# Decoder LSTM step with the doubled cell in PSUM and one transposed block per step; order of the first loads changed

## The chip, the cores and the metric

One core of a Trainium2 chip runs the whole program. The time is the device time of one execution in microseconds (us), the median of several runs. TensorE (PE) multiplies matrices into PSUM, PEld is its weight load, VectorE (DVE) and ScalarE (ACT) work on tiles in SBUF and PSUM, GpSimd (POOL) on tiles in SBUF, and SyncE (SP) issues the DMAs of this kernel. Each engine works through its own queue in order; semaphores tie the queues together.

## What is computed

```python
h = tok(x)                          # x: 16 x 1024 x 64; token mixing
h = h + attn(layernorm(h))          # LSTM encoder (both directions) and LSTM decoder
h = h + ffn(layernorm(h))           # 8 experts, the 2 best of each token

def tok(x):                         # q, k, v = x @ W + b
    y = ((d_gamma * (q @ k.T)) @ v) @ Wo + bo
    return where(y >= 0, y, prelu_a * y)

def step(carry, xw):                # of each LSTM, 1024 steps, 16 x 128 state
    h, c = carry
    i, f, g, o = split(xw + h @ U, 4, axis=-1)
    c = sigmoid(f) * c + sigmoid(i) * tanh(g)
    h = sigmoid(o) * tanh(c)
    return (h, c), h

h_fwd, h_bwd = lstm(x @ Wf + bf, Uf), lstm(x @ Wb + bb, Ub, reverse=True)
dec = lstm(broadcast(concat(h_fwd, h_bwd)) @ Wd + bd, Ud, return_sequences=True)
attn_out = dec @ Wo + bo
```

The experts compute gelu(x @ W1 + b1) @ W2 + b2, masked by the two best gate scores.

## The kernel before, in words

The program is four blocks that follow each other; an engine enters a block only when all engines have left the one before.

**Set-up** (`setup`, L163). SP issues the gamma matrix (L195), the weights of token mixing, `bo_col` and `a_col` (L202 to L204), four bias rows, and then 22 loads of weights for the later stages (`load_raw`, L208 to L230), which count on `m.s_raw`. TensorE turns gamma, ScalarE keeps it (L272), and VectorE splits the weights of token mixing into high and low halves and makes the bias rows (L290 to L299). VectorE and TensorE wait for `s_w`, which counts all small loads up to `a_col`.

**Token mixing** (`token_mixing`, L374) goes through the 16 batches. SP loads x of batches 0 and 1 (L446), then x of batch b + 2 and the store of h of batch b in turn (L448 to L452). ScalarE's `x_split` (L598) is the first operation on a batch's x. A batch's 16 places `t` interleave the main part (`gate`, L626), the preparation of the next batch (`prep`) and the layernorm of the last one (`post`). `bo_col` is read at L580 and `a_col` at L644. GpSimd meanwhile waits for all 22 weights (L457) and splits them (`split_weights`, L334); the encoder needs them.

**Encoder** (`encoder`, L815): two chains, forward and backward, take turns for 1024 steps.

**Decoder and experts** (`decoder_and_experts`, L934): one chain of 1024 steps, in 32 bodies of `BODY` = 32 steps, all unrolled. A step of the chain is: twelve products of 16 columns on TensorE (`pe_gates`: eight of the high half of h, L749, then four of the low half, L752), tanh of the gates (L760, L762) on ScalarE, terms (L775) and their sum, twice the cell (L781), on VectorE, tanh of the cell (L767) on ScalarE, which writes PSUM bank 3, and back on VectorE h as a float16 high half (L806), as float32 (L807) and the low half (L812). `dve_rest` (L795) has the output gate (L798) and `dve_half_cell` (L792), which halves the doubled cell for the next step's terms. `twice_cell` is an SBUF tile.

Beside the chain, the experts of the tokens that earlier bodies made are worked through in tiles of 32 steps' tokens. A tile j has places s = 0 to 63 and starts in the body after its own; in a body the tile of the body before is at places 0 to 31 and the one before that at 32 to 63. `pe_part`, `act_part`, `in_tanh` and `in_gates` say what an engine does at a place. `in_tanh` stands in VectorE's order before the high half, `in_gates` behind the low half. At s = 37 and 38, which are steps 5 and 6 of a body, TensorE turns the sums yT, two blocks each (L1137), one float32 block being two matmuls in the trace. VectorE reads them at s = 43 (L1316). After its tile's work in each step TensorE runs a number of products that nobody reads (`pe_idle`, L740; `idle_products`, L921), which keep it busy.

```python
    by_place = {0: 0, 1: 4, 2: 5, 19: 5, 20: 9}
```

gives that number for the steps in which tiles are in work, save steps 3 to 18, which have 10 or 13.

## Time and profile before

| what | value |
|---|---|
| median of 3 runs | 3925.51 us (3924.63 to 3928.59) |
| profiled run | 3921.38 us, span 3919.6 us |
| PE busy | 3750.3 us (96%) |
| PEld busy | 2749.2 us (70%) |
| DVE busy | 3139.5 us (80%) |
| ACT busy | 2391.9 us (61%) |
| POOL busy | 85.4 us (2%) |
| set-up, token mixing | 0 to 26.3, 26.3 to 398 us |
| encoder, decoder | 398 to 2141, 2141 to 3919.6 us |

Busy time is the time in which an engine had an instruction of its own; DMA-issuing and waiting don't count. TensorE's share holds the products that nobody reads (15583 of 61932 matmuls are of L740), so it is not a measure of useful work. PEclk in the windows is the granted share of 2.4 GHz. A row of the timeline has start, duration, engine, line, operation and tiles, how many instructions were merged, and in brackets the idle time of the engine before it with what ended it.

### The profile page before, as it was taken

The numbers are of one execution on the slowest core, as the hardware profiler recorded it, in microseconds if no ns is written. First come the engines' busy times: TensorE is split into PE (matmuls) and PEld (weight loads), VectorE is DVE, ScalarE is ACT, GpSimd is POOL, SyncE is SP. The second block draws the span as 40 slices with busy tenths as digits, with TensorE's granted clock in tenths as the row PEclk, the third lists the DMA queues.
The fourth block names the chain that finished last, engine by engine and source line by source line (L and its number), as shares of the span: only waits on it lengthen the run. The fifth ranks groups of instructions, "written<-read, shape, count | busy, mean of one in ns | idle before, by whom it ended". The sixth has DMA issues, their size and how long they took to land. (4 is left out here: it accounts for less than half of the span.)

```text
span 3919.6 us, 159989 instructions
## 1 busy us (share of the span) xinstructions
PE 3750.3 (96%) x61932; PEld 2749.2 (70%) x61932; DVE 3139.5 (80%) x21227; ACT 2391.9 (61%) x11882; POOL 85.4 (2%) x129
## 2 busy tenths in 40 slices
PE   7899999999999999999999899999999999999998
PEld 3333888888888888888888666666666666666664
DVE  6999899999999999999998677766777667776675
ACT  3232898888889889888887344444444443444443
POOL 6100000000000000000000000000000000000000
PEclk8999999999999999999999999999999999999999
DMA  3111000000000000000000000000000000000000
GB/s 91 22 25 23 3 3 3 3 3 3 3 3 3 3 3 3 3 3 3 3 3 4 4 8 8 8 6 6 8 8 8 6 7 7 8 8 6 6 8 7
DMA packets 49571, 34.01 MB, mean 9 GB/s; under 512 B 37661, under 2 KB 46877, under 8 KB 48806
## 3 DMA queue, kind: packets, MB, share of 16 engines
q1 hardware_dynamic: 48806, 23.77, 2.3%
q8 instruction: 485, 7.95, 0.8%
q14 instruction: 280, 2.29, 0.2%
HBM read 15.37 MB, written 8.39 MB: 6 GB/s over the span
## 5 line engine op out<-in xcount | busy, mean ns | idle before, releaser
L740 PE MATMUL bank<-xs,ident 128*128 128x128 f16 x15583 | 1415.1, 223 | 0.0
L740 PEld LDWEIGHTS bank<-xs,ident 128*128 128x128 f16 x15583 | 1010.2, 102 | 252.2 <-issue 229.8
L760 ACT ACTIVATE ifg_cell_dec<-bank 128x48 f32<-128x48 f32 x1024 | 215.2, 210 | 641.3 <-PE bank L752 641.3
L752 PE MATMUL bank<-enc_lo,u_hi 128*128 128x16 f16 x8192 | 530.1, 173 | 0.3 <-DVE enc_lo L812 0.3
L749 PE MATMUL bank<-enc_hi,u_lo 128*128 128x16 f16 x8192 | 527.8, 173 | 0.0
L775 DVE SCALAR_TENSOR_TENSOR terms_dec<-ifg_cell_dec 128x32 f32<-128x32 f32 x1024 | 197.1, 193 | 398.3 <-ACT ifg_cell_dec L760 387.2
L749 PE MATMUL bank<-enc_hi,u_hi 128*128 128x16 f16 x8192 | 501.6, 170 | 0.0
L749 PEld LDWEIGHTS bank<-enc_hi,u_lo 128*128 128x128 f16 x8192 | 338.4, 96 | 205.6 <-DVE enc_hi L806 171.2
L767 ACT ACTIVATE bank<-twice_cell_dec 128x16 f32<-128x16 f32 x1024 | 191.7, 187 | 402.4 <-DVE twice_cell_dec L781 402.4
L752 PEld LDWEIGHTS bank<-enc_lo,u_hi 128*128 128x128 f16 x8192 | 339.3, 96 | 67.9 <-DVE enc_lo L812 0.4
L749 PE MATMUL bank<-ring_hi,u_lo 128*128 128x16 f16 x4096 | 260.7, 172 | 102.3 <-DVE ring_hi L806 96.0
L749 PEld LDWEIGHTS bank<-enc_hi,u_hi 128*128 128x128 f16 x8192 | 349.5, 96 | 0.0
L786 ACT ACTIVATE out_gate_bwd<-tanh_o_bwd,encoder_half_scale 128x16 f32<-128x16 f32 x1024 | 315.1, 308 | 33.6
L786 ACT ACTIVATE out_gate_fwd<-tanh_o_fwd,encoder_half_scale 128x16 f32<-128x16 f32 x1024 | 315.1, 308 | 33.5
L854 PE MATMUL bank<-ones,bias 128*128 128x128 bf16 x1024 | 323.4, 316 | 0.0
L852 PE MATMUL bank<-xs,w_lo 128*128 128x128 f16 x1024 | 323.2, 316 | 0.0
L749 PEld LDWEIGHTS bank<-ring_hi,u_lo 128*128 128x128 f16 x4096 | 183.6, 97 | 181.4 <-DVE ring_hi L806 160.5
L850 PE MATMUL bank<-xs,w_hi 128*128 128x128 f16 x1024 | 278.1, 272 | 1.4 <-PEq L434 1.4
L752 PE MATMUL bank<-ring_lo,u_hi 128*128 128x16 f16 x4096 | 263.6, 173 | 0.6 <-DVE ring_lo L812 0.3
L749 PE MATMUL bank<-ring_hi,u_hi 128*128 128x16 f16 x4096 | 250.6, 170 | 0.0
L1128 PE MATMUL bank<-hid,w 128*64 128x512 f32 x448 | 240.2, 618 | 0.0
L767 ACT ACTIVATE bank<-twice_cell_bwd 128x16 f32<-128x16 f32 x1025 | 191.8, 187 | 53.9
(268 smaller groups left out, 7900.8 us busy)
## 6 DMA issues: line engine op xcount, KB each, us to landing
g_rows<-tok_d_gamma_batched_dram SPq DMA_DIRECT2D x8, 512.0 KB, 6.5
x_rows<-in_x_dram SPq DMA_DIRECT2D x16, 256.0 KB, 3.0
kept_h<-tok_ln_h SPq DMA_DIRECT2D x32, 128.0 KB, 2.1
res<-kept_h SPq DMA_DIRECT2D x32, 128.0 KB
out_dram<-sums SPq DMA_DIRECT2D x32, 128.0 KB
raw_wd<-in_L_attn_Wd_dram SPq DMA_DIRECT2D x2, 256.0 KB
raw_experts<-in_L_ffn_W_dram SPq DMA_DIRECT2D x2, 256.0 KB
raw_u<-in_L_attn_Uf_dram SPq DMA_DIRECT2D x1, 256.0 KB
```

Of the source, the lines that this page charges most:

```text
L740: nc.tensor.matmul(spare, m.ident16[:], m.xs[:, 0, :, :].rearrange("p b t -> p (b t)"), start=False, stop=True, skip_group_check=True)
L749: nc.tensor.matmul(z[k], w[:, g, :], h_hi, start=False, stop=False, skip_group_check=True)
L752: last = nc.tensor.matmul(z[k], m.u_hi[c.d][:, g, :], h_lo, start=False, stop=True, skip_group_check=True)
L760: nc.scalar.activation(c.ifg_cell[:, 0:3, :], ifg, ACT.Tanh, scale=1.0 / Z_SCALE).then_inc(c.s_t_ifg, 1)
L767: nc.scalar.activation(c.tanh_cell, c.twice_cell[:], ACT.Tanh, scale=0.5).then_inc(c.s_tanh_cell, 1)
L775: nc.vector.scalar_tensor_tensor(c.terms[:], c.ifg_cell[:, 0:2, :], 1.0, c.ifg_cell[:, 2:4, :], ALU.add, ALU.mult).then_inc(c.s_terms, 1)
L786: nc.scalar.activation(c.out_gate[:], c.tanh_o[:], ACT.Identity, scale=0.5 * X_SCALE, bias=half_scale).then_inc(c.s_out_gate, 1)
L850: nc.tensor.matmul(z, m.w_hi[d][:, g, :], x, start=(k in (0, 3)), stop=False, skip_group_check=True)
L852: nc.tensor.matmul(z, m.w_lo[d][:, g, :], x, start=False, stop=False, skip_group_check=True)
L854: nc.tensor.matmul(z, m.lstm_bias[d][:, GATE_FROM[g], :], m.ones3[:].rearrange("p (b t) -> p b t", b=B), start=False, stop=False, skip_gro ...
L1128: mm(y_bank[0:D, :], m.w2[:, e, :], hid[:, e % 2, :], start=False, stop=False, skip_group_check=True)
```

## The change

1. In the decoder alone, `twice_cell` becomes columns 16 to 31 of PSUM bank 3, beside the cell's tanh in columns 0 to 15. VectorE's sum writes it there; ScalarE's tanh and VectorE's halving read it there.
2. In the decoder, the halving no longer stands behind the output gate but between h in float32 (L807) and the low half (L812).
3. The four blocks of yT are turned at s = 37, 38, 39 and 40, one each.
4. In step 19 of a body with tiles TensorE runs 2 products that nobody reads instead of 5.
5. x of batches 0 and 1 is loaded in the set-up behind the four bias rows. `bo_col`, `a_col` and the 22 weights are issued at the start of token mixing, ahead of x of batch 2; the first readers of `bo_col` and `a_col` wait for a semaphore of their own.

```diff
+def load_x(nc, sp, m, b, k):
+    sp.dma_start(m.x_rows[k][:], m.a["x"][b, 0].rearrange("(c p) d -> p c d", p=P)).then_inc(m.s_x[k], 16)
+def load_weights(nc, sp, m):
+    a = m.a
+    for k in range(2):
+        sp.dma_start(m.bo_col[k * D:(k + 1) * D, :], a["L0_tok_bo"][:, None]).then_inc(m.s_cols, 16)
+    sp.dma_start(m.a_col[:], a["L0_tok_prelu_a"][None, :].broadcast_to([P, 1])).then_inc(m.s_cols, 16)
...
+N_RAW = 16 * 22
@@ -199,36 +243,11 @@
-                for k in range(2):
-                    load(m.bo_col[k * D:(k + 1) * D, :], a["L0_tok_bo"][:, None])
-                load(m.a_col[:], a["L0_tok_prelu_a"][None, :].broadcast_to([P, 1]))
                 for k, name in enumerate(("bq", "bq", "bk", "bk")):
                     load(raw_mix[:, k * D:(k + 1) * D], a["L0_tok_" + name][None, :].broadcast_to([3, D]), s_b, n_b)
...
+                for b in range(2):
+                    load_x(nc, sp, m, b, b)
@@ -434,27 +452,23 @@
-                for b in range(2):
-                    load(b, b)
+                load_weights(nc, sp, m)
                 for b in range(B):
                     if b + 2 < B:
                         sp.wait_ge(s_xs, b + 1)
-                        load(b + 2, b % 2)
+                        load_x(nc, sp, m, b + 2, b % 2)
                     store_h(b)
@@ -577,6 +591,8 @@
                         act.wait_ge(s_av, NT * (b + 1))
+                        if b == 0:
+                            act.wait_ge(m.s_cols, 48)
@@ -641,6 +657,8 @@
                         dve.wait_ge(s_y, b + 1)
+                        if b == 0:
+                            dve.wait_ge(m.s_cols, 48)
@@ -715,20 +733,21 @@
-    def __init__(self, sb, sem, d, name, cell_bank):
+    def __init__(self, sb, sem, d, name, cell_bank, twice_in_bank=False):
         self.d = d
         self.tanh_cell = cell_bank[:, 0:B]
+        self.twice_cell = cell_bank[:, B:2 * B] if twice_in_bank else sb(f"twice_cell_{name}", [P, B], F32)[:]
@@ -789,15 +808,14 @@
-def dve_rest(nc, dve, c, n, sums):
+def dve_out_gate(nc, dve, c, n):
 
     dve.wait_ge(c.s_t_o, n + 1)
     nc.vector.tensor_scalar(c.out_gate[:], c.tanh_o[:], 1.0, 0.5 * X_SCALE, ALU.add, ALU.mult
                             ).then_inc(c.s_out_gate, 1)
-    dve_half_cell(nc, dve, c, sums)
@@ -922,7 +940,7 @@
-    by_place = {0: 0, 1: 4, 2: 5, 19: 5, 20: 9}
+    by_place = {0: 0, 1: 4, 2: 5, 19: 2, 20: 9}
@@ -940,7 +958,7 @@
-        c = Chain(sb, sem, 2, "dec", m.bank[3])
+        c = Chain(sb, sem, 2, "dec", m.bank[3], twice_in_bank=True)
@@ -1130,14 +1148,14 @@
-                    if s in (37, 38):
+                    if 37 <= s < 37 + QS:
 
                         if s == 37:
                             pe.wait_ge(s_yT, j + 1)
-                        for blk in range(2 * (s - 37), 2 * (s - 37) + 2):
-                            last = mm(pre_bank[0][:, blk * D:(blk + 1) * D], yT[:, blk * P:(blk + 1) * P],
-                                      m.ident[0:D, 0:D], start=(blk == 0), stop=True, skip_group_check=True)
-                        if s == 38:
+                        blk = s - 37
+                        last = mm(pre_bank[0][:, blk * D:(blk + 1) * D], yT[:, blk * P:(blk + 1) * P],
+                                  m.ident[0:D, 0:D], start=(blk == 0), stop=True, skip_group_check=True)
+                        if blk == QS - 1:
                             last.then_inc(s_yt, 1)
@@ -1359,11 +1377,12 @@
                         dve_terms(nc, dve, c, n)
                         dve_sum(nc, dve, c, n)
-                        dve_rest(nc, dve, c, n, n + 1)
+                        dve_out_gate(nc, dve, c, n)
                         part(in_tanh, tiles, step)
                         dve.wait_ge(c.s_tanh_cell, n + 1)
                         dve.wait_ge(c.s_out_gate, n + 1)
                         dve_hidden(nc, dve, c, n, h_at(ring_hi, n))
+                        dve_half_cell(nc, dve, c, n + 1)
                         dve_hidden_low(nc, dve, c, n, h_at(ring_hi, n), h_at(ring_lo, n))
                         part(in_gates, tiles, step)
```

## Rows read from the trace of the kernel before

**Rows 1.** Window, decoder: us; PE, PEld, DVE, ACT, POOL busy; clock; DMA; GB/s.

```profile
2141.10:3881.30 1740.20, 1636.83 (x24968) 1142.34 (x24968) 1217.75 (x8279) 699.48 (x3472) 0.00 (x0) 0.99 0.03 7
```

**Rows 2.** Timeline of ScalarE in a plain step of the decoder, and the next step's start.

```profile
3757.67 0.21 ACT L760 ACTIVATE ifg_cell_dec<-bank 128x48 f32<-128x48 f32 x1 [0.82 <-PE bank L752]
...
3758.35 0.19 ACT L767 ACTIVATE bank<-twice_cell_dec 128x16 f32<-128x16 f32 x1 [0.39 <-DVE twice_cell_dec L781]
...
3759.36 0.21 ACT L760 ACTIVATE ifg_cell_dec<-bank 128x48 f32<-128x48 f32 x1 [0.22 <-PE bank L752]
```

**Rows 3.** Timeline of VectorE in the same step, from the sum on.

```profile
3758.14 0.17 DVE L781 TENSOR_TENSOR twice_cell_dec<-terms_dec 128x16 f32<-128x16 f32 x1
...
3758.57 0.17 DVE L806 TENSOR_TENSOR ring_hi<-out_gate_dec,bank 128x16 f16<-128x16 f32 x1
3758.66 0.16 DVE L807 TENSOR_TENSOR h_dec<-out_gate_dec,bank 128x16 f32<-128x16 f32 x1
3758.85 0.18 DVE L812 TENSOR_TENSOR ring_lo<-h_dec,ring_hi 128x16 f16<-128x16 f32 x1
```

**Rows 4.** Source view of ScalarE's lines: shortest/median/longest ns, first and last start.

```profile
L767 ACT ACTIVATE bank<-twice_cell_dec x1024: 187/187/188, 2144.1 to 3881.6; 128x16 f32<-128x16 f32 x171
...
L762 ACT ACTIVATE tanh_o_dec<-bank x1024: 178/178/179, 2143.4 to 3881.0; 128x16 f32<-128x16 f32 x171
...
L583 ACT ACTIVATE tok_ln_dev<-tok_ln_var x16: 208/208/209, 72.3 to 392.4; 128x8 f32<-128x8 f32 x16
```

**Rows 5.** Timeline of step 5 of a body, ScalarE and TensorE.

```profile
3728.90 0.21 ACT L760 ACTIVATE ifg_cell_dec<-bank 128x48 f32<-128x48 f32 x1 [0.31 <-PE bank L752]
...
3730.62 0.21 ACT L760 ACTIVATE ifg_cell_dec<-bank 128x48 f32<-128x48 f32 x1 [0.85 <-PE bank L752]
...
3729.01 0.66 PE L1138 MATMUL bank<-ident,ff_yT 64*128 64x64 f32 x4
```

**Rows 6.** Timeline of step 19 of the same body, ScalarE and TensorE.

```profile
3752.54 0.21 ACT L760 ACTIVATE ifg_cell_dec<-bank 128x48 f32<-128x48 f32 x1 [0.21 <-PE bank L752]
...
3754.29 0.21 ACT L760 ACTIVATE ifg_cell_dec<-bank 128x48 f32<-128x48 f32 x1 [0.88 <-PE bank L752]
...
3753.54 0.45 PE L740 MATMUL bank<-xs,ident 128*128 128x128 f16 x5
3753.83 0.25 PE L749 MATMUL bank<-ring_hi,u_lo 128*128 128x16 f16 x4
...
3754.03 0.24 PE L752 MATMUL bank<-ring_lo,u_hi 128*128 128x16 f16 x4
```

**Rows 7.** Window on the second of ten stretches of the decoder at half clock.

```profile
3130.20:3133.60 3.40, 3.40 (x54) 3.40 (x52) 2.44 (x20) 0.80 (x6) 0.00 (x0) 0.51 0.00 0
```

**Rows 8.** Timeline of SP in the set-up and at token mixing's start.

```profile
12.38 0.36 SPq L191 DMA_DIRECT2D raw_u<-in_L_attn_Uf_dram  x1
...
25.43 0.27 SPq L191 DMA_DIRECT2D raw_b<-in_L_ffn_b_dram  x1
26.30 4.98 SPq L438 DMA_DIRECT2D x_rows<-in_x_dram  x3
```

**Rows 9.** Timeline of ScalarE in the set-up and at token mixing's start.

```profile
16.29 0.19 ACT L275 COPY bv<-bv 64x3 f32<-64x3 f32 x1 [0.67 <-PE bank L260]
...
29.41 0.63 ACT L598 ACTIVATE x_split<-x_rows 128x512 f16<-128x512 f32 x1 [1.61 <-DMA x_rows<-in_x_dram]
```

**Rows 10.** Timeline of VectorE, its last operation in the set-up.

```profile
21.59 0.48 DVE L331 TENSOR_TENSOR bias<-left 3x320 bf16<-3x320 f32 x1
```

**Rows 11.** Timeline of GpSimd's first split, and of a small VectorE operation.

```profile
27.57 0.54 POOL L310 TENSOR_SCALAR raw_u<-raw_u 128x128 f32<-128x128 f32 x1 [23.68 <-DMA raw_b<-in_L_ffn_b_dram]
...
105.89 4.20 DVE L677 TENSOR_SCALAR tok_ln_t<-tok_ln_t 128x8 f32<-128x8 f32 x1
```

**Rows 12.** Windows from x_split to x_split, two batches of token mixing.

```profile
81.71:120.81 39.10, 23.63 (x121) 8.05 (x120) 36.91 (x38) 6.72 (x12) 33.34 (x15) 0.83 0.06 14
120.81:141.38 20.57, 20.57 (x123) 7.51 (x121) 19.06 (x36) 6.75 (x13) 0.00 (x0) 1.00 0.12 27
```

More of the change, by code:

```diff
@@ L156, in build @@
             m.s_raw = raw_sem("raw_loaded")
+            m.s_cols = raw_sem("columns_loaded")
+            m.s_b2 = raw_sem("b2_zeroed")
+            m.x_rows = [raw_sb(f"x_rows{k}", [P, NB, D], F32) for k in range(2)]
+            m.s_x = [raw_sem(f"x_loaded{k}") for k in range(2)]
             setup(nc, m)
@@ L160, in build, with load_raw @@
         decoder_and_experts(nc, m)
+def load_x(nc, sp, m, b, k):
[5 more added lines that the diff above has]
+    sp.dma_start(m.a_col[:], a["L0_tok_prelu_a"][None, :].broadcast_to([P, 1])).then_inc(m.s_cols, 16)
+    def load_raw(dst, src, scattered=False):
+        sp.dma_start(dst, src, allow_slow_non_contiguous=scattered).then_inc(m.s_raw, 16)
+    for d, u in enumerate((a["L0_attn_Uf"], a["L0_attn_Ub"], a["L0_attn_Ud"])):
+        load_raw(m.raw_u[d][:], u)
+    for d, w in enumerate((a["L0_attn_Wf"], a["L0_attn_Wb"])):
+        load_raw(m.raw_w[d][0:D, :], w)
+        load_raw(m.raw_w[d][D:2 * D, :], w)
+    for d in range(2):
+        load_raw(m.raw_wd[d][:], a["L0_attn_Wd"][H * d:H * (d + 1), :])
+    load_raw(m.raw_wo[:], a["L0_attn_Wo"])
+    for k in range(2):
+        load_raw(m.raw_wg[k * D:(k + 1) * D, :], a["L0_ffn_Wg"])
+        load_raw(m.raw_w1[k * D:(k + 1) * D, :, :], a["L0_ffn_W1"].rearrange("e d h -> d e h"))
+    load_raw(m.w2[:], a["L0_ffn_W2"].rearrange("e h d -> h e d"))
+    load_raw(m.b1[:], a["L0_ffn_b1"].rearrange("e h -> h e"), scattered=True)
+    at = 0
+    for name in ("attn_bf", "attn_bb", "attn_bd", "attn_bo", "ffn_bg"):
+        b = a["L0_" + name]
+        load_raw(m.raw_b[:, at:at + b.shape[0]], b[None, :].broadcast_to([3, b.shape[0]]))
+        at += b.shape[0]
+    sp.wait_ge(m.s_b2, 1)
+    load_raw(m.raw_b2[E:2 * E, 0, :], a["L0_ffn_b2"])
+N_RAW = 16 * 22
 def setup(nc, m):
@@ L386, in token_mixing @@
     with ctx:
-        x_rows = [sb(f"x_rows{k}", [P, NB, D], F32) for k in range(2)]
+        x_rows, s_x = m.x_rows, m.s_x
         x_split = sb("x_split", [P, NB, 2 * D], F16)
@@ L402, in token_mixing @@
         ln = Layernorm(sb, "tok_ln_")
-        s_x = [sem(f"x_loaded{k}") for k in range(2)]
         s_xh, s_xs, s_xt, s_xk, s_vo, s_vk, s_tile, s_hi, s_lo = (sem(n) for n in (
@@ L436, in _ @@
             def _(sp):
-                def load(b, k):
-                    sp.dma_start(x_rows[k][:], a["x"][b, 0].rearrange("(c p) d -> p c d", p=P)).then_inc(s_x[k], 16)
                 def store_h(b):
@@ L711 @@
 class Chain:
-    def __init__(self, sb, sem, d, name, cell_bank):
+    def __init__(self, sb, sem, d, name, cell_bank, twice_in_bank=False):
         self.d = d
         self.tanh_cell = cell_bank[:, 0:B]
+        self.twice_cell = cell_bank[:, B:2 * B] if twice_in_bank else sb(f"twice_cell_{name}", [P, B], F32)[:]
         self.ifg_cell = sb(f"ifg_cell_{name}", [P, 4, B], F32)
         self.terms = sb(f"terms_{name}", [P, 2, B], F32)
-        self.twice_cell, self.tanh_o, self.out_gate, self.h = (
-            sb(f"{part}_{name}", [P, B], F32) for part in ("twice_cell", "tanh_o", "out_gate", "h"))
+        self.tanh_o, self.out_gate, self.h = (
+            sb(f"{part}_{name}", [P, B], F32) for part in ("tanh_o", "out_gate", "h"))
         (self.s_z_ifg, self.s_z_o, self.s_t_ifg, self.s_t_o, self.s_terms, self.s_out_gate, self.s_twice,
@@ L729, in start @@
     def start(self, nc, own):
-        own.link(nc.vector.memset(self.twice_cell[:], 0.0))
+        own.link(nc.vector.memset(self.twice_cell, 0.0))
         nc.vector.memset(self.ifg_cell[:, 3, :], 0.0).then_inc(self.s_cell, 1)
```

40 lines of the change are left out of this document (8 added, 32 removed).

## The prediction

> **What bounds the kernel now.** I read the windows by stage first. Token mixing, encoder and decoder follow one another, and the decoder takes 1740.2 us of the 3919.6 us span [rows 1]. The diff touches two places: the decoder's step, and the order of loads around the set-up. The encoder keeps its instructions, and its tiles stay where they were; I put it at no change.
>
> In the decoder I read one step on three engines. ScalarE starts two successive tanh of the gates 1.69 us apart [rows 2]. 1024 steps at 1.69 us are 1730 us, so the loop through time is the stage. The loop runs so: gates' tanh (L760), terms (L775), their sum (L781), tanh of the cell (L767), hidden state high (L806) and in float32 (L807), its low half (L812), then TensorE's four products of the low half (L752), then the next gates' tanh. TensorE looks 94% busy [rows 1], but most of that is filler (L740). In the plain step the sum starts at 3758.14 and lasts 0.17, the cell's tanh starts at 3758.35 and lasts 0.19, and the high half starts at 3758.57: every link starts 0.03 to 0.04 after the end of the one before [rows 2, 3]. So a nanosecond off any of these durations is a nanosecond off the step, as long as TensorE is not what comes last.
>
> **Part 1, the doubled cell in PSUM.** The sum now writes PSUM, the cell's tanh and the halving (L792) read PSUM. ScalarE's tanh has three forms in the trace: from SBUF to PSUM 16 columns 187 ns, from PSUM to SBUF 16 columns 178, from SBUF to SBUF 8 columns 208 [rows 4]. The 48-column gates' tanh takes 0.21 and the 16-column one 0.178, so 32 columns are 0.03 and 8 columns some 7 ns [rows 2, 4]: SBUF to SBUF with 16 columns would be 215. Reading PSUM thus saves 215 - 178 = 37 ns where the output is SBUF; writing PSUM saves 28. If the savings added, PSUM to PSUM would take 150. They may overlap: the bounds for the tanh are 141 (a saving of 46, some more than the larger of the two) and 187 (none). I take 154, a saving of 33, a little below the sum of the parts.
>
> No row shows VectorE writing PSUM. Nearest are its reads: the high half has an input in PSUM and takes 0.17, as the sum with both in SBUF does [rows 3]; for VectorE one memory is as near as the other when it reads. I take 0 for the write, and bound it by -10 ns (the 0.17 of the sum against the 0.16 of L807) and by +37, ScalarE's largest gap turned round. Together: 33 ns a step, bounds 56 and -4. 1024 x 33 = 33.8 us.
>
> ScalarE's reading agrees with a rule that I set beside the rows: the Trainium skill (VectorE: DVE Perf Modes, section on the TRN2 errata) gives ScalarE 224 cycles from SBUF and 172 from PSUM, 43 ns at its 1.2 GHz; by that the 33.8 would be 44. The same table gives VectorE 62 cycles (65 ns) more from PSUM than from SBUF, which the 0.17 of L806 against the 0.17 of L781 contradicts.
>
> **Part 2, the halving moves.** It leaves the gap between out_gate and the high half and stands between L807 and L812. Where it was it cost nothing: it ran beside the tanh, and the high half started 0.22 after it, on the tanh's end [rows 3]. Its steps with an operation of in_tanh have the same gap, now with more room. Where it goes there is a gap too: L812 starts 0.20 after L807, because it waits for L807's end, while VectorE issues two such small operations 0.09 apart (L806 to L807) [rows 3]. The halving would start 0.09 behind L807 and let L812 go 0.18 behind it, so 0.02 stays spare: cost 0. Its result is wanted by the next terms, some 0.7 us later. Behind it queue L812 and all of in_gates; who waits for L812 is TensorE, on the path. That is the thin place.
>
> **Part 3, one block of transposes a step.** Now steps 5 and 6 of a body carry two blocks each. Step 5 takes 1.72 us from tanh to tanh, against 1.69; the four matmuls of its two blocks last 0.66 us, at about 0.13 each, 0.26 a block [rows 5]. TensorE then reaches the gates late. The median excess over the bodies is 34 ns in step 5 and 18 in step 6. A block less takes 0.26 away, more than either lateness; both excesses go. Steps 7 and 8 get the block; their filler ends some 0.5 us before the high half is there, so 0.26 is hidden. 30 bodies x 52 ns = 1.6 us. The sum of sums (L1316, step 43) comes three steps after the last block: no cost.
>
> **Part 4, three fillers fewer in step 19.** That step takes 1.75 us, 62 ns above the others. Five fillers last 0.45, so one is 56 ns, and the gates' first product starts 0.29 behind the start of the five [rows 6]. Against the chain (0.24 + 0.23 + 0.21 + 0.22 + 0.17 + 0.06 = 1.13 from tanh to first product if TensorE is free, all from [rows 2, 3] but the last, which is the wait's own) it starts at 1.29: 0.16 late. Three fillers are 0.168. The excess goes: 31 bodies x 62 ns = 1.9 us.
>
> **Where TensorE takes over.** The eight products of the high half take 0.20 [rows 6], and those of the low half can't start until 0.35 after the high half's end, so TensorE may start up to about 0.15 behind that end at no cost. The rest are medians over the bodies, each taken as in [rows 5, 6] from a step's L806, L749 and the two L760 around it: late by 0.144, step 2 loses 4 ns; late by 0.191, step 5 loses 34; the excess is the lateness less 0.157. A chain that is 33 ns shorter makes each TensorE-late step later by 33: steps 23 and 31 (now 0.132) then lose 8 each, step 2 loses 20, the others with 0.10 or 0.09 nothing. 36 ns x 31 = 1.1 us given back. **Decoder: 33.8 + 1.6 + 1.9 - 1.1 = 36.2 us.** With 56 ns it is 57.6, with 0 it is 3.5.
>
> **Part 5, the granted clock.** Ten times in the decoder, from 2642.0 to 3676.3 us, the clock is granted at 1.2 GHz instead of 2.4 for 3.4 us [rows 7]. All ten begin in step 6, right behind both pairs of transposes, and each makes that step 0.47 to 0.72 us longer, 6.2 us in all. The transposes use 64 rows and 64 columns. Spread over four steps, with the fillers of steps 5 and 6 no longer pushed back, that thin stretch is gone: 6.2 us, bounds 0 and 6.2.
>
> **Part 6, the loads.** Before, SP issues bo_col and a_col, then 22 weights from 12.38 to 25.70, and the next block starts at 26.30 with x's load, for which ScalarE waits until 29.41 [rows 8, 9]. After, x is issued from about 10.5, and the set-up ends with VectorE's last bias row, now 22.07 [rows 10]. That moves up too: a_col was the last load waited for. ScalarE stood idle 0.67 before L275 [rows 9], so the gain is 0.67 at most; I take 0.6, and the set-up ends at 21.45. With 0.60 between blocks (25.70 to 26.30) token mixing starts at 22.05. ScalarE's table load and first operation come first; it waited 1.61 for x behind them [rows 9]. x_split starts at 22.05 + (29.41 - 1.61 - 26.30) = 23.55 against 29.41: **5.9 us**.
>
> What is moved behind: the three columns and 22 weights issue from 22.05 to about 37.2; GpSimd, which began 2.1 us after the last issue (27.57), begins at 39.1, 11.5 us later, and ends near 128, long before the encoder at 398. On SP's queue, x of batch 2 now stands behind them, issued at 37.3 and landed at 40.1; ScalarE wants it at 52.2 (12 us of cover, the whole cost if that were gone). The first store of h (66.4) is not reached. bo_col lands near 25 and is read near 57. GpSimd's long operations block small VectorE ones: a scale of 8 columns takes 4.20 us beside one [rows 11], and the batch under them takes 39.10 us against 20.57 for the next [rows 12]. They shift by 11.5 us late and the batches by 5.9 early; about as many small operations meet them. I put it at 0, between -5 and +6.
>
> **Sum.** 36.2 + 6.2 + 5.9 = 48.3. The profiled run took 3921.4 us (span 3919.6), and comes to 3873.1. The median of the runs shown is 4.1 higher, 3925.5; on it: 3877.2.
>
> **The rivals.** *A: VectorE pays for PSUM what ScalarE saves.* With +37 on the sum a step gains -4 ns, the decoder loses 4.1 and keeps 3.5, so 3925.5 + 0.6 - 12.1 = 3914. For it: no row shows the write. Against: the equal reads. The Trainium skill (ScalarE: Activation LUTs, where it compares destinations) has this rule: "ScalarE is closer to PSUM, VectorE is closer to SBUF." No row here shows its second half for a write. Chance 0.17.
>
> *B: TensorE is the bound in the 14 steps with late products.* If their margin were not 0.157 but what they use now, 13 of them would gain nothing: 13 x 33 x 31 = 13.3 us less, 3891. Against: step 23, late by 0.132, is as short as the rest. Chance 0.06.
>
> *C: the low half slips, and it is slower.* If VectorE doesn't issue L812 until the halving has ended, L812 starts 0.09 + 0.17 + 0.03 = 0.30 after L807, not 0.20: 99 ns, less 33, are 66 ns a step, 67.6 us; less 15.6 for the other parts, 3978. It decides from a slip of 48 ns. For it: L812 is on the path and has 20 ns to spare. Against: L807 is issued 0.09 after L806, not after its end. Chance 0.07.
>
> *D: the change does less than it says*: the half clock stays, or the blocked batch grows: 6 us each, 3883 to 3890; these are inside the forecast's case.
>
> **How the numbers follow.** Forecast 0.64 (3858 to 3893), A 0.17, B 0.06, C 0.07, something else 0.06, split between faster and slower. The range goes from the larger saving (57.6 + 6.2 + 5.9 = 69.7, so 3856) to A: 3857 to 3914. The likeliest case's own range is 3858 to 3893. 0.2% (7.9 us, about what a measurement of this kernel tells from no change) puts the line at 3917.6: faster 0.86, same 0.05, slower 0.09.
>
> **What would show it.** L767 at about 154 ns (178 or more: part 1 is wrong); L781 still 174, and ScalarE starting 0.21 behind it (0.24 is A); L812 0.20 behind L807 (0.30 is C); steps 5, 6 and 19 as short as the rest, near 1.655; no half clock after a transposing step; first x_split at 23.5; the third batch still near 39 us. The prediction is wrong if the write isn't near 0, or if a different VectorE operation ends last in the step.

## The result, and the profile after

| | before | after |
|---|---|---|
| median of the runs timed side by side, us | 3925.07 (4 runs, 3919.37 to 3928.59) | 3901.52 (4 runs, 3894.48 to 3902.35) |
| ratio, 95% interval | 1 | 0.9933 [0.9917, 0.9948] |
| profiled execution, us; its span | 3921.38; 3919.6 | 3894.48; 3892.7 |
| mean granted TensorE clock | 0.986 | 0.992 |
| first x_split starts, us | 29.41 | 23.36 |
| encoder's first gates' tanh | 403.54 | 394.34 |
| decoder, first to last gates' tanh | 1737.58 | 1719.25 |

The kernel is 23.6 us faster by the medians and 26.9 by the two profiled spans, where 48.3 had been forecast. Each part gained as its sign said, and the total was half. 3901.5 lies inside the whole range (3857 to 3914) and above the likeliest case's own (3858 to 3893).

The first row of the page after answers to the table that stands ahead of the prediction (engine, busy us, share of the span, instructions):

```profile
PE 3752.8 (96%) x61839; PEld 2740.7 (70%) x61839; DVE 3054.7 (78%) x21227; ACT 2367.2 (61%) x11882; POOL 86.9 (2%) x129
```

The window on the decoder after, columns as in [rows 1]: it is 17.9 us shorter than [rows 1], and ScalarE is busy 25 us less for the same 3472 instructions.

```profile
2132.50:3854.80 1722.30, 1639.04 (x24874) 1135.86 (x24874) 1134.95 (x8281) 674.80 (x3472) 0.00 (x0) 1.00 0.03 7
```

**The plain step.** Timeline of ScalarE after (start, duration, engine, line, output and input, idle time before and what ended it), which answers to [rows 2]:

```profile
3730.35 0.21 ACT L779 ACTIVATE ifg_cell_dec<-bank 128x48 f32<-128x48 f32 x1 [0.23 <-PE bank L771]
...
3731.04 0.17 ACT L786 ACTIVATE bank<-bank 128x16 f32<-128x16 f32 x1 [0.40 <-DVE bank L800]
...
3732.02 0.21 ACT L779 ACTIVATE ifg_cell_dec<-bank 128x48 f32<-128x48 f32 x1 [0.82 <-PE bank L771]
```

Timeline of VectorE in the same step, which answers to [rows 3]:

```profile
3730.82 0.18 DVE L800 TENSOR_TENSOR bank<-terms_dec 128x16 f32<-128x16 f32 x1
...
3731.24 0.17 DVE L824 TENSOR_TENSOR ring_hi<-out_gate_dec,bank 128x16 f16<-128x16 f32 x1 [0.16 <-ACT bank L786]
3731.32 0.16 DVE L825 TENSOR_TENSOR h_dec<-out_gate_dec,bank 128x16 f32<-128x16 f32 x1
3731.41 0.17 DVE L811 TENSOR_SCALAR ifg_cell_dec<-bank 128x16 f32<-128x16 f32 x1
3731.52 0.18 DVE L830 TENSOR_TENSOR ring_lo<-h_dec,ring_hi 128x16 f16<-128x16 f32 x1
```

Gates' tanh to gates' tanh takes 1.67 where it took 1.69. From the sum's start to the tanh of the cell it is now 0.22 (0.21 before), from there to the high half 0.20 (0.22 before). The halving (L811) stands 0.09 behind the float32 hidden state, and the low half still starts 0.20 behind that. The source views give the nanoseconds (shortest/median/longest; first and last start), the tanh (L786) and the sum (L800), with the encoder's unchanged pair as a yardstick in the same run:

```profile
L786 ACT ACTIVATE bank<-twice_cell_fwd x1024: 187/187/188, 395.0 to 2129.1; 128x16 f32<-128x16 f32 x171
L786 ACT ACTIVATE bank<-bank x1024: 168/168/168, 2135.9 to 3855.1; 128x16 f32<-128x16 f32 x171
```

```profile
L800 DVE TENSOR_TENSOR twice_cell_fwd<-terms_fwd x1024: 174/175/178, 394.8 to 2128.9; 128x16 f32<-128x16 f32 x171
...
L800 DVE TENSOR_TENSOR bank<-terms_dec x1024: 182/182/185, 2135.7 to 3854.9; 128x16 f32<-128x16 f32 x171
```

The tanh has lost 19 ns (187 to 168) and the sum has gained 8 (174 to 182). That leaves about 10 ns a step: the median step is 1675 ns, where it was 1685.

**Steps 5 and 19.** ScalarE's gates' tanh of steps 5, 6 and 7 of a body, and of steps 19 and 20 of the same one. They answer to [rows 5, 6]; each step is now as long as a plain one, 1.67:

```profile
3757.15 0.21 ACT L779 ACTIVATE ifg_cell_dec<-bank 128x48 f32<-128x48 f32 x1 [0.33 <-PE bank L771]
3758.82 0.21 ACT L779 ACTIVATE ifg_cell_dec<-bank 128x48 f32<-128x48 f32 x1 [0.82 <-PE bank L771]
3760.50 0.21 ACT L779 ACTIVATE ifg_cell_dec<-bank 128x48 f32<-128x48 f32 x1 [0.82 <-PE bank L771]
...
3780.60 0.21 ACT L779 ACTIVATE ifg_cell_dec<-bank 128x48 f32<-128x48 f32 x1 [0.23 <-PE bank L771]
3782.27 0.21 ACT L779 ACTIVATE ifg_cell_dec<-bank 128x48 f32<-128x48 f32 x1 [0.82 <-PE bank L771]
```

**The loads.** SP's queue after, which answers to [rows 8]:

```profile
10.71 1.04 SPq L168 DMA_DIRECT2D x_rows<-in_x_dram  x2
21.96 1.12 SPq L175 DMA_DIRECT2D bo_col<-in_L_tok_bo_dram  x2
...
36.18 0.27 SPq L179 DMA_DIRECT2D raw_b<-in_L_ffn_b_dram  x1
36.49 0.39 SPq L168 DMA_DIRECT2D x_rows<-in_x_dram  x1
```

Then ScalarE's and VectorE's last operations of the set-up and the first of token mixing, and GpSimd's first; they answer to [rows 9 to 11]:

```profile
15.69 0.19 ACT L294 COPY bv<-bv 64x3 f32<-64x3 f32 x1 [0.24 <-PE bank L279]
...
20.98 0.48 DVE L350 TENSOR_TENSOR bias<-left 3x320 bf16<-3x320 f32 x1
...
23.36 0.61 ACT L614 ACTIVATE x_split<-x_rows 128x512 f16<-128x512 f32 x1
...
38.56 0.54 POOL L329 TENSOR_SCALAR raw_u<-raw_u 128x128 f32<-128x128 f32 x1 [34.66 <-DMA raw_b<-in_L_ffn_b_dram]
```

x is in the queue at 10.71, ScalarE no longer waits for it, and the first x_split starts at 23.36, 6.05 us earlier. GpSimd starts 11.0 later. The windows from x_split to x_split answer to [rows 12] (same columns): the blocked batch and the next one. The blocked one is now the fifth interval instead of the fourth.

```profile
95.34:132.61 37.27, 24.47 (x122) 8.18 (x121) 35.71 (x38) 6.73 (x12) 32.23 (x14) 0.82 0.07 15
132.61:153.06 20.45, 20.45 (x122) 7.46 (x121) 19.06 (x36) 6.74 (x12) 0.00 (x0) 1.00 0.12 26
```

And the timeline's row for VectorE's worst operation of 8 columns in the blocked one, usually 0.17 us:

```profile
118.32 4.20 DVE L695 TENSOR_SCALAR tok_ln_t<-tok_ln_t 128x8 f32<-128x8 f32 x1
```

GpSimd's row beside it starts before it and ends at 122.50; VectorE's ends at 122.52:

```profile
118.16 4.34 POOL L349 TENSOR_SCALAR bias_left<-bias_part,ident 3x1608 f32<-3x1608 bf16 x1
```

**The balance by the two traces**, in us of span, forecast beside it. The decoder's rows are sums over its steps from the second body on, of what each took beyond the median step:

| part | forecast | measured |
|---|---|---|
| median step, 1023 steps | -33.8 | -10.2 (1685 to 1675 ns) |
| steps 5, 6 and 19, less what TensorE gives back | -2.4 | -3.2 |
| steps under a half-clock stretch | -6.2 | -6.7 (6.8 to 0.1) |
| single steps more than 0.1 us longer than the median | 0 | +1.6 (13 to 23 of them) |
| loads, first x_split | -5.9 | -6.05 |
| intervals of token mixing | 0 | -2.7 |
| end of token mixing, encoder, tail and rounding | 0 | +0.3 |
| sum | -48.3 | -26.9 |

### The profile page after: what moved, and what is told of

Same layout as the page of the kernel before. It is cut to its first block and busy times, and to the rows that moved or that the text cites. A ratio compares the mean times of both kernels' runs of the same rounds, so it can differ in the third digit from the quotient of the medians.

```text
span 3892.7 us, 159805 instructions
## 1 busy us (share of the span) xinstructions
PE 3752.8 (96%) x61839; PEld 2740.7 (70%) x61839; DVE 3054.7 (78%) x21227; ACT 2367.2 (61%) x11882; POOL 86.9 (2%) x129
## 5 line engine op out<-in xcount | busy, mean ns | idle before, releaser
L759 PE MATMUL bank<-xs,ident 128*128 128x128 f16 x15490 | 1397.8, 221 | 0.0
L759 PEld LDWEIGHTS bank<-xs,ident 128*128 128x128 f16 x15490 | 994.6, 101 | 256.3 <-issue 230.0
L786 ACT ACTIVATE bank<-bank 128x16 f32<-128x16 f32 x1024 | 172.0, 168 | 411.7 <-DVE bank L800 411.7
L805 ACT ACTIVATE out_gate_fwd<-tanh_o_fwd,encoder_half_scale 128x16 f32<-128x16 f32 x1024 | 315.1, 308 | 33.6
L824 DVE TENSOR_TENSOR ring_hi<-out_gate_dec,bank 128x16 f16<-128x16 f32 x1024 | 174.7, 171 | 147.9 <-ACT bank L786 133.4
```

The lines of the kernel that those rows point to most:

```text
L759: nc.tensor.matmul(spare, m.ident16[:], m.xs[:, 0, :, :].rearrange("p b t -> p (b t)"), start=False, stop=True, skip_group_check=True)
L786: nc.scalar.activation(c.tanh_cell, c.twice_cell, ACT.Tanh, scale=0.5).then_inc(c.s_tanh_cell, 1)
L805: nc.scalar.activation(c.out_gate[:], c.tanh_o[:], ACT.Identity, scale=0.5 * X_SCALE, bias=half_scale).then_inc(c.s_out_gate, 1)
L824: tt(h_hi, c.out_gate[:], c.tanh_cell, ALU.mult).then_inc(c.s_hi, 1)
```

## The experiments

Two theories were set against each other for the missing 21 us. **Theory 1:** the two savings of the tanh overlap, and VectorE pays some nanoseconds to write PSUM; the other parts do what was forecast. **Theory 2 (the rival):** the step gained more, and another wait took it back: the moved halving, or TensorE. Two more questions were why the half clock went, and what GpSimd's later start does. Each comparison is with runs of the kernel before on the same chip. The kernels whose names begin with p_ have a part of the change alone, the others start from after. Medians are of all executions of a kernel; every row and every count of steps or stretches is of its one profiled execution.

**The doubled cell in PSUM and the moved halving alone (p_psum), and the moved halving alone (p_half).**

```
 # p_half: before, with the halving behind the hidden state
-                        dve_rest(nc, dve, c, n, n + 1)
+                        dve_out_gate(nc, dve, c, n)
                         dve_hidden(nc, dve, c, n, h_at(ring_hi, n))
+                        dve_half_cell(nc, dve, c, n + 1)
                         dve_hidden_low(...)
 # p_psum: the same, and
-        c = Chain(sb, sem, 2, "dec", m.bank[3])
+        c = Chain(sb, sem, 2, "dec", m.bank[3], twice_in_bank=True)
```

> The kernel before with the decoder's doubled cell in PSUM and the halving between L807 and L812; transposes, filler and loads as before. Theory (a step gets shorter by what the cell's tanh saves less what the sum pays): tanh 168 ns, sum 182 ns, a plain step 1.675 us instead of 1.685, so about 10 us less, minus what steps 5, 6, 19, 2, 23 and 31 give back because TensorE is late there; 3915 to 3917. Rival (the gain comes from moving the halving, not from PSUM): the step is 1.675 also with the doubled cell in SBUF, see p_half. The half clock after the pairs of transposes stays under both theories, in about as many bodies.

> The kernel before with only the halving moved between L807 and L812, the doubled cell still in SBUF. Theory: nothing moves, tanh 187 ns, L812 0.198 us after L807, step 1.685 us. Rival (the move itself is worth the 10 ns): step 1.675 us. Rival C of the prediction (the low half slips): L812 0.3 us after L807 and a step of 1.78.

p_psum: 3917.09 us (10 runs) against 3923.7 of before (25 runs), ratio 0.9988 [0.9978, 0.9997], at the upper end of what was expected. The tanh takes 168 ns, the sum 182, the median step 1676. Ten half-clock stretches stay, as in before, all in step 6. p_half (one run): 3925.8, tanh 187, sum 174, low half 198 ns behind the float32 state, median step 1685. So the step's 10 ns come from PSUM alone, and moving the halving costs the plain step nothing. It does cost something else: the number of single steps more than 0.1 us longer than the median, half-clock ones aside, goes from 13 in before to 26 in p_half and 25 in p_psum, and what they take from 3.4 us to 5.7 and 5.8. That is the larger part of why p_psum's decoder is only 6.4 us shorter, not 9.2 to 10.2 (9 to 10 ns by 1023); 0.6 us more goes to steps 5, 6 and 19, where TensorE is late. The single long steps are looked at under the encoder's experiment.

**One block of transposes per step alone (p_turns), and the change with the pairs put back (a_pairs).**

```
 # shortened. p_turns: before, with the change's turns (a_pairs: the reverse, in after)
-                    if s in (37, 38):
+                    if 37 <= s < 37 + QS:
-                        for blk in range(2 * (s - 37), 2 * (s - 37) + 2):
+                        blk = s - 37
```

> The kernel before with only the four blocks of yT turned one a step (s = 37 to 40); step 19 keeps its 5 fillers, the chain its SBUF tile. Theory (the pairs of transposes are what the half clock follows): none of the ten stretches at half clock is left, steps 5 and 6 are as short as the plain ones, step 19 still 1.747: 6.2 + 1.6 = 7.8 us less. Rival (the shorter step or the other order of loads moved the bodies against the clock's decisions): some of the ten stay and only 1.6 us go.

> The changed kernel with yT turned in pairs again (s = 37, 38); all else as changed. Theory (the half clock went because three edits act together: blocks spread, a shorter step, another time of the bodies): with the pairs back, stretches at half clock follow step 6 again in several bodies, steps 5 and 6 are 40 and 25 ns longer than the plain 1.675, and the kernel takes 6 to 9 us more than the changed one. Rival (it was the shorter step and the loads alone, the blocks don't matter to the clock): no stretch at half clock in the decoder, 2 us more.

p_turns: 3923.05 us (10 runs), ratio 0.9998 [0.9989, 1.0007]. Steps 5 and 6 are plain again where the clock is full (1.689 and 1.687 against 1.718 and 1.702). But five half-clock stretches stay, and all begin in step 6 although no step carries a pair. The window on one of them (columns as in [rows 7]):

```profile
3242.20:3245.60 3.40, 3.40 (x42) 3.26 (x40) 2.63 (x21) 0.66 (x4) 0.00 (x0) 0.50 0.00 0
```

Timeline of ScalarE's gates and TensorE's transposes around it:

```profile
3241.57 0.43 PE L1138 MATMUL bank<-ident,ff_yT 64*128 64x64 f32 x2
3241.65 0.21 ACT L760 ACTIVATE ifg_cell_dec<-bank 128x48 f32<-128x48 f32 x1 [0.82 <-PE bank L752]
...
3243.51 0.69 PE L1138 MATMUL bank<-ident,ff_yT 64*128 64x64 f32 x2
3243.59 0.21 ACT L760 ACTIVATE ifg_cell_dec<-bank 128x48 f32<-128x48 f32 x1 [1.07 <-PE bank L752]
...
3246.00 0.21 ACT L760 ACTIVATE ifg_cell_dec<-bank 128x48 f32<-128x48 f32 x1 [1.55 <-PE bank L752]
```

The granted clock is 0.50, which is the 1.2 GHz level, and steps 6 and 7 last 1.94 and 2.41 us. One stretch now costs 0.98 us, where it cost about 0.62 with the pairs: a block of step 7 falls under the half clock too (0.69 us for its two instructions instead of 0.43). Expected were 7.8 us less, or 1.6 by the rival. The profiled decoder is 3.0 us shorter, and the median over the executions moves by 0.65 us, with an interval (3.5 us less to 2.7 more) that rules out the 7.8 and not the 1.6. The stretches stay, as the rival has it. a_pairs: 3901.45 us (4 runs), 0.9952 [0.9935, 0.9968], six stretches in step 6 again, profiled decoder 5.6 us longer than after's. Of it 3.7 are the stretches and 1.9 the late steps 5 and 6. By the medians a_pairs is 3.9 us slower than after_again, less than the 6 to 9 that were expected.

**The change with the doubled cell back in SBUF (a_sbuf), and again as it is (after_again).**

```
 # a_sbuf
-        c = Chain(sb, sem, 2, "dec", m.bank[3], twice_in_bank=True)
+        c = Chain(sb, sem, 2, "dec", m.bank[3])
```

> The changed kernel with the decoder's doubled cell in SBUF again; halving, blocks, fillers and loads as changed. Theory: tanh 187, sum 174, step 1.685, 10 us more than the changed kernel from the step, and some stretches at half clock back, as in the kernel before with only the blocks spread, 3 us more; 3911 to 3915. Rival (the step's length has no part in the half clock): exactly the 10 us, 3911, no half clock in the decoder.

> The changed kernel itself, beside the versions below and beside the kernel before on the same chip. Theory: 0.993 of the kernel before, no stretch at half clock in the decoder between its first and last body, third to fifth batch of token mixing together about 19 us above 3 x 20.45. Rival (that no half clock stands in the decoder was one lucky execution): two to six such stretches and a mean granted clock of 0.988 over the executions.

a_sbuf: 3911.04 us (10 runs), 0.9978 [0.9969, 0.9988]. Its profiled execution was the slowest of the ten (3919.70), so its rows are less typical than the others'. Tanh 187, sum 175, median step 1688 (3 ns more than before's, for which no row gives a reason). Five half-clock stretches are back, all in step 6, and they cost 5.6 us, although no step carries a pair of transposes. after_again: 3897.51 (4 runs), 0.9942 [0.9925, 0.9958], median step 1675, one stretch.

One stretch at the start of the second body (6.8 us, in p_psum 10.2) is in every kernel, the prediction's ten don't count it, and nothing here moves it. From the third body to the last, before has 10 stretches and p_psum 10; p_half, p_turns and a_sbuf have 5, p_loads and a_pairs 6; after has none and after_again one. Neither the shorter step alone (p_psum) nor the spread turns alone (p_turns) takes them away, and with either missing (a_pairs, a_sbuf) five or six are back. The two together do. The unprofiled executions bear it out: taken over all of a kernel's executions, the mean granted clock has its median at 0.991 and 0.990 in after and after_again, at 0.988 in a_pairs and a_sbuf, and at 0.986 to 0.987 in before, p_psum, p_turns, p_half and p_loads. Why is open: in every kernel each of these stretches begins in step 6, but most bodies pass it at full clock. In before they come in series 54.6 us apart, which is the length of a body with a stretch in it (one without takes 54.0). That points to how the body falls against something periodic, and this is argued, not shown.

**The loads alone (p_loads).**

```
 # p_loads: after, with the decoder's turns, fillers, halving and SBUF cell of before
 ...
-    by_place = {0: 0, 1: 4, 2: 5, 19: 2, 20: 9}
+    by_place = {0: 0, 1: 4, 2: 5, 19: 5, 20: 9}
```

> The kernel before with only the loads changed: x of batches 0 and 1 in the set-up, the two columns and 22 weights at token mixing's start. Theory: the first x_split at 23.4 us instead of 29.4, the encoder's first tanh of the gates at 394.3 instead of 403.5, 9 us less. Rival (the set-up gives 6 and the rest of the 9 is chance of one execution): 6 us less.

3917.31 us (10 runs), 0.9985 [0.9976, 0.9994], 6.4 us less than before; the interval goes from 2.4 to 9.4 us and so excludes neither the 9 nor the rival's 6. In the profiled execution x_split starts at 23.02, 6.4 us earlier than in before, and the encoder's first tanh at 395.49, 8.0 us earlier. The other 1.7 us are in token mixing's intervals: together they took 315.8 to 317.2 us in the four kernels with the old order of loads and 313.7 to 315.1 in the eight with the new one and GpSimd's work uncut.

**A second halving (a_two_halves).** It adds one instruction whose result nobody reads.

```
                         dve_half_cell(nc, dve, c, n + 1)
+                        nc.vector.tensor_scalar(c.spare[:], c.twice_cell, 0.5, None, ALU.mult)
                         dve_hidden_low(...)
```

> The changed kernel with a second halving, into a tile that nobody reads, right behind the first, between L807 and L812. Theory (VectorE issues such operations about 0.085 apart whatever their length, and the place between h and its low half holds one but not two): L812 starts 3 x 0.085 = 0.26 us after the float32 write instead of 0.198, a step of 1.735, 60 us more in all. Rival (the place holds any number, since the low half waits for something else): no difference. Other rival (each waits for the one before to end): L812 at 0.45 and 250 us more.

3943.56 us (one run), 46.0 more than after_again, where 60 were expected; decoder 1764.80 against 1719.73. Timeline of VectorE in one step:

```profile
3001.28 0.16 DVE L826 TENSOR_TENSOR h_dec<-out_gate_dec,bank 128x16 f32<-128x16 f32 x1
3001.37 0.17 DVE L812 TENSOR_SCALAR ifg_cell_dec<-bank 128x16 f32<-128x16 f32 x1
3001.45 0.16 DVE L1387 TENSOR_SCALAR spare_dec<-bank 128x16 f32<-128x16 f32 x1
3001.53 0.17 DVE L831 TENSOR_TENSOR ring_lo<-h_dec,ring_hi 128x16 f16<-128x16 f32 x1
```

VectorE issues these 0.08 to 0.09 apart, and the low half starts 0.25 behind the hidden state instead of 0.20: with one operation in the gap there is room, with two there isn't. The median step grows by 38 ns: 49 of later start, less 11 by which the low half itself is shorter (164 instead of 175 ns). That the low half gets shorter was not foreseen. The single long steps grow from 23 to 45. So the gap of the forecast was real, and it is used up by one operation.

**The forms by themselves (forms).** A block of 16-column operations that depend on one another, between encoder and decoder, adds them to the work.

```
 # tiles' slices shortened; VectorE's five loops are left out
+                for dst, src in ((a_dst, a_src), (pb, a_src), (a_dst, pa), (pb2, pa), (pa2, pa)):
+                    for _ in range(8):
+                        own.link(S.activation(dst, src, ACT.Tanh, scale=0.5))
```

> The changed kernel with a block between encoder and decoder that runs five forms of a 16-column tanh on ScalarE and five of a 16-column add on VectorE, eight times each, every one waiting for the one before. Theory (the saving of reading PSUM and that of writing it overlap, whichever banks are used): tanh SBUF to SBUF 210 to 215 ns, SBUF to PSUM 187, PSUM to SBUF 178, PSUM to PSUM 168 both in one bank and across banks; add into SBUF 174, into PSUM 182. Rival (168 and not 150 because ScalarE reads and writes the same bank 3): across banks 150.

Groups by form of the added block (busy us, mean ns; fa_, fd_ are in SBUF, bank is PSUM), ScalarE and then VectorE:

```profile
L874 ACT ACTIVATE bank<-bank 128x16 f32<-128x16 f32 x16 | 2.7, 168 | 0.5
L874 ACT ACTIVATE fa_dst<-fa_src 128x16 f32<-128x16 f32 x8 | 1.7, 215 | 1.9 <-DVE fa_dst L853 1.7
L874 ACT ACTIVATE bank<-fa_src 128x16 f32<-128x16 f32 x8 | 1.5, 187 | 0.3
L874 ACT ACTIVATE fa_dst<-bank 128x16 f32<-128x16 f32 x8 | 1.5, 183 | 0.3
...
L858 DVE TENSOR_TENSOR bank<-fd_src 128x16 f32<-128x16 f32 x8 | 1.5, 182 | 0.3
L862 DVE TENSOR_TENSOR bank<-fd_src,bank 128x16 f32<-128x16 f32 x8 | 1.4, 178 | 0.3
L864 DVE TENSOR_TENSOR bank<-fd_src,bank 128x16 f32<-128x16 f32 x8 | 1.4, 178 | 0.3
L856 DVE TENSOR_TENSOR fd_dst<-fd_src 128x16 f32<-128x16 f32 x8 | 1.4, 172 | 0.3
L860 DVE TENSOR_TENSOR fd_dst<-fd_src,bank 128x16 f32<-128x16 f32 x8 | 1.4, 170 | 0.3
```

ScalarE: 215 ns from SBUF to SBUF, 187 to PSUM, 183 from PSUM, 168 with both. One move saves 28 or 32, the second one only 19 or 15 more. VectorE: 172 from SBUF to SBUF, 182 when it writes PSUM, 170 when one input is in PSUM. Writing costs 10, reading nothing. Whether source and result share a bank makes no difference (x16 at 168 are both cases of ScalarE, L862 and L864 those of VectorE). Three of these are the step's numbers to 2 ns, without the step (187, 168 and 182); PSUM to SBUF is 183 here and 178 in the step's L762. The rival, the shared bank, is out, and theory 1 stands for the step. Of theory 2 the 1.6 us of single long steps are left, and they are small beside what is missing.

**GpSimd's work in smaller pieces (a_chunks).**

```
-    split_in_place(engine, own, m.w1_hi[:], m.w1_lo[:], m.raw_w1[:], W_SCALE)
+    for e in range(E):
+        split_in_place(engine, own, m.w1_hi[:, e, :], m.w1_lo[:, e, :], m.raw_w1[:, e, :], W_SCALE)
-    bias_rows(engine, own, m, m.bias[0:3, 0:BIAS_MIX], m.raw_b[:], part, left)
+    for at in range(0, BIAS_MIX, 201):
+        cols = slice(at, at + 201)
+        bias_rows(engine, own, m, m.bias[0:3, cols], m.raw_b[:, cols], part[:, :, cols], left[:, :, cols])
```

> The changed kernel with GpSimd's longest work cut up: the experts' weights split one expert at a time, the bias rows 201 columns at a time. Theory (a small VectorE operation waits until the GpSimd operation beside it has ended, so the 19 us that the batches lose are as long as GpSimd's operations are): no VectorE operation of 8 columns above 1 us, the batches lose 4 to 8 us instead of 19, 11 to 15 us less than the changed kernel. Rival (the loss goes by GpSimd's busy time, which grows with the number of operations): as long or longer.

3875.94 us (4 runs), 0.9888 [0.9874, 0.9903], 21.6 less than after_again on the same chip, where 11 to 15 were expected: the fastest kernel here. Windows of the fourth and of the sixth interval (columns as in [rows 12]):

```profile
72.50:92.95 20.45, 20.40 (x121) 7.46 (x121) 19.46 (x37) 6.83 (x13) 18.31 (x43) 1.00 0.12 26
...
113.50:134.39 20.89, 20.73 (x121) 7.26 (x121) 19.88 (x37) 6.85 (x13) 18.52 (x30) 1.00 0.12 26
```

GpSimd is as busy here as in the blocked batch, 18.52 of 20.89 us against 32.23 of 37.27, and yet TensorE keeps its full clock and the interval is 0.4 longer than the plain 20.45. GpSimd ends at 158 instead of 129, still long before the encoder. From the third on the intervals are 21.35, 20.45, 20.55, 20.89, 20.86 and then 20.45, and no VectorE operation is longer than its usual time by more than 0.42 us. So the rival, GpSimd's busy time, is out: what hurt was the length of its single operations. In after, the five VectorE operations of 8 columns that took the longest (0.52 to 4.20 us) each ended 0.03 us behind the end of a GpSimd operation, as the two rows under the blocked batch's window show for one. The wide ones, of 512 columns, were stretched too, by up to 3.3 us, and what ends those is not shown. The encoder starts 19.5 us earlier.

**The encoder's doubled cell in PSUM too (a_enc), and both (best).**

```
-        ch = [Chain(sb, sem, d, name, m.bank[6 + d]) for ...
+        ch = [Chain(sb, sem, d, name, m.bank[6 + d], twice_in_bank=True) for ...
-                        dve_terms(nc, dve, ch[d], n, own_cell=False)
+                        dve_terms(nc, dve, ch[d], n)
-                        dve_half_cell(nc, dve, ch[d], n + 1 + d)
+                        if n or d:
+                            dve_half_cell(nc, dve, ch[late], n + 1)
```

> The changed kernel with the doubled cell in PSUM in the encoder too; the halving of a chain stands behind the other chain's sum, so that VectorE reads that chain's bank when ScalarE has left it. Theory (the encoder's loop goes through the same tanh and sum): tanh 187 to 168, sum 175 to 183, 8 to 10 ns less for each of 1024 steps, 8 to 10 us less. Rival (the encoder is bound by ScalarE's order or TensorE's fillers, which a shorter tanh doesn't touch): no difference.

> Both of the two before together. Theory: their savings add, 19 to 25 us less than the changed kernel, 0.987 to 0.988 of the kernel before. Rival (one of them gives nothing): 0.990 to 0.991.

a_enc: 3907.55 us (6 runs), 0.9966 [0.9954, 0.9978], 10.0 slower than after_again; the encoder takes 1742.65 us instead of 1734.26. best: 3887.65 (4 runs), 0.9917 [0.9902, 0.9931], 11.7 slower than a_chunks. Neither the theory (8 to 10 us less) nor the rival (no difference) foresaw a loss. The encoder's tanh is 168 ns too, but its median step is 1696 against 1695, so the shorter tanh gains nothing there; that it is off the path because the two chains share ScalarE and VectorE is argued, not shown. What it loses is in three steps of every 64, which are 0.06, 0.16 and 0.23 us longer. (The encoder that nobody changed takes 1732.3 to 1739.1 us in the other kernels' profiles, so of the 8.4 us some may be the execution's own; the medians, 10.0 and 11.7 apart, are clear of that.) Timeline of VectorE in the longest one:

```profile
732.75 0.16 DVE L825 TENSOR_TENSOR h_fwd<-out_gate_fwd,bank 128x16 f32<-128x16 f32 x1
733.10 0.19 DVE L794 SCALAR_TENSOR_TENSOR terms_bwd<-ifg_cell_bwd 128x32 f32<-128x32 f32 x1 [0.18 <-issue]
```

The terms start 0.35 behind the operation before, where a usual half step has 0.11, and what ended VectorE's idle time is "issue", no other engine. The decoder's single long steps are of the same kind. In after, step 146 starts the halving 0.29 behind the float32 state, not 0.09:

```profile
2381.70 0.16 DVE L825 TENSOR_TENSOR h_dec<-out_gate_dec,bank 128x16 f32<-128x16 f32 x1
2381.99 0.17 DVE L811 TENSOR_SCALAR ifg_cell_dec<-bank 128x16 f32<-128x16 f32 x1
```

They recur every 188 steps (59, 247, 435; 122, 310, 498; 223, 411, 599, 787), at the same step numbers in before (122, 310, 498; 223, 411, 599, 787) and in most kernels, whatever the time. What they go by is VectorE's own count. In the encoder and, from the second body on, the decoder of the fourteen kernels, half-clock stretches left out, 304 starts of a VectorE instruction come more than 0.15 us later behind the one before than such a pair usually has, 0.15 to 0.35 us. All 304 are at the same place of 128 in VectorE's sequence, waits counted: 188 steps of the decoder are 1920 instructions, 15 x 128, and 64 steps of a_enc's encoder 896, 7 x 128. In forms, where 49 more VectorE instructions stand ahead of the decoder, all these series lie 33 steps later, and still at that place of 128. Most of the places cost nothing, since VectorE would have waited there anyway: after's decoder has about 80, of which 23 make a long step.

The DMA rows of the page suggest what the place is. The queue q14 carries instructions, 8 KB a transfer (transfers, MB, share of 16 engines), in after, a_enc and a_two_halves:

```profile
q14 instruction: 280, 2.29, 0.2%
...
q14 instruction: 296, 2.42, 0.2%
...
q14 instruction: 288, 2.36, 0.2%
```

a_enc's edit adds a wait to each half step, 2048 instructions in all, and 16 transfers; a_two_halves adds 1024 instructions and 8 transfers. That is one for every 128. So VectorE pauses where it passes from one such block of its code to the next, and the pause costs only where it meets the path. That it waits for the transfer itself is not shown. With the halving moved, one more instruction stands between the cell's tanh and the low half, and ten more pauses meet it. In the encoder none of 92 such places came late in any kernel without a_enc's edit: at 12 VectorE instructions a step they fall on the same three instructions all the time, and at 14 on seven.

## Why the prediction was half right

- **Part 1, the step that failed.** The tanh was taken at 154 and takes 168: two savings that were read singly in [rows 4] (37 and 28 by the forecast's own reading) were nearly added, with 154 "a little below the sum". The forms show that they overlap, 215 - 168 = 47 for both together, 32 and 28 for each. The write of the sum was taken at 0 and costs 8; the argument was that VectorE's reads are equal in both memories, which forms confirms (172 and 170), but a read says nothing of a write (182). 14 ns and 8 ns by 1023 steps are 22.5 us; the row of the median step in the balance falls short by 23.6, and the other rows together come out 2.2 better than forecast, which leaves the 21.4 that are missing. By its own signs, too, this part was off: 168 lies between its 154 and its 178, and the write isn't near 0. Both values lay within the bounds of the text, but the lower end of the sum did not hold what it says: -4 ns pairs the dearest write (+37) with the full 33 of the tanh, and with the tanh's own lower end, no saving, it would be -37. ScalarE's 32 ns for a source in PSUM instead of SBUF (215 to 183) have the sign, and three quarters of the size, of the 43 that come out of the cycles in the Trainium skill (VectorE: DVE Perf Modes, section on the TRN2 errata), while its 65 ns more for VectorE's reads of PSUM are contradicted once more, by 170 against 172.
- **The rule behind rival A.** "ScalarE is closer to PSUM, VectorE is closer to SBUF" (the Trainium skill, ScalarE: Activation LUTs) had no row for its second half. Now it has: the trace agrees in sign, 8 ns in the step and 10 in the block of forms, about a quarter of the 37 that the rival supposed. The forecast took the memories as equal although this rule gave the write a sign.
- **Part 2** was right for the plain step: the low half stays 198 ns behind the state, and a_two_halves shows that the room is one operation wide. It missed 1.6 us of pauses that the moved instruction brings onto the path: the forecast has no term for single long steps, though before had 13.
- **Parts 3 and 4, TensorE's give-back.** Steps 5, 6 and 19 are plain, 3.2 us. The 1.1 us given back wasn't there, since the step shrank by 10 ns and not by 33: lateness in steps 23 and 31 went from 0.132 to 0.142, below the 0.157.
- **Part 5**, the half clock: the amount was right (6.7 against 6.2), the cause was not. "Right behind both pairs" named the place and took it for the cause; with the pairs spread and nothing else (p_turns) five stretches stay and each costs more. It went only where the shorter step and the spread turns came together, for a reason that is open, so the right amount was luck; and a second profile of after had one stretch again, worth 1.0 us.
- **Part 6**, the loads: x_split at 23.36 against 23.55, block start at 21.96 against 22.05, GpSimd at 38.56 against 39.1. The blocked batches gained 2.4 us, within its -5 to +6, and the 37 us batch is one place further on than the forecast had it.
- **Rivals.** The result, 3901.5, is between the forecast's 3877 and A's 3914. A held by a quarter. B is out as far as 10 ns a step can test it: the steps with late products are as short as the others. C is out: 198 ns, not 300. Of D, the blocked batch didn't grow, and the half clock went in one profile of after and left one stretch in the other.

## What to carry to other kernels

When an operation's source and destination both move to another memory, don't add two savings that were each read with the other end in SBUF, and don't infer a write from a read: a block of eight dependent operations of each form settles it in one run. Before shifting a long engine's work about, look at the length of its single operations: cutting GpSimd's wide splits and bias rows into pieces was worth 21.6 us, nearly as much as the whole change. And an instruction or a wait added to a long unrolled loop can cost more than its slot: it moves the places, one in every 128 instructions, at which VectorE pauses, and can bring them onto the path.

## What the runs showed of the hardware that was not expected

- A 16-column tanh on ScalarE: 215 ns SBUF to SBUF, 187 to PSUM, 183 from PSUM, 168 with both. A 16-column add on VectorE: 172, and 182 to PSUM, 170 with one input in PSUM.
- A VectorE operation of 8 columns that meets a long GpSimd operation lasts up to 4.2 us for 0.17, until the GpSimd operation ends, and with GpSimd equally busy in short operations at most 0.42 us longer than usual.
- VectorE pauses for up to 0.35 us at one place in every 128 of its instructions, waits counted (304 of 304 late starts over 0.15 us), and the trace has one 8 KB transfer of instructions for every 128. Whether the pause waits for that transfer is open.
- From the decoder's third body on the granted clock falls to the 1.2 GHz level (for 3.4 us, once for 6.8) only in step 6 of a body, in 0 to 10 of 30 bodies, and changes of 10 ns a step or of one transpose a step move that number; the cause is open.
